# Attention in 16 heads: side work dealt out between the three fills of a head, and the rows of maxima issued on ScalarE's queue

## The chip, the cores and the metric

The kernel runs on one core of a Trainium2 chip. The metric is the device time in microseconds from start to end of one execution; the time before is the median of three runs.

## The reference, cut to what matters

The whole program is two transformer-like layers over x of shape (16, 512, 256). The change touches only the second layer's attention (16 batches, 512 tokens, 16 heads of width 16):

```python
h = _layernorm(x) * (1 + ca) + sa
qkv = (h @ w_qkv).reshape(Bx, Tx, 3, H, HD)
scores = einsum('bhqd,bhkd->bhqk', q, k) * SCALE      # causal mask to -inf
scores = scores + head_scales * (q[..., :8] @ dir) * (k[..., :8] @ dir)
attn = softmax(scores); out = attn @ v
x = x + ga * (out @ w_out)
```

## The kernel before, in words

`attention_stage` writes one program for each engine by hand; the engines meet only at semaphores, and each executes its own list in order. `Signal` objects count events: `pe.wait_ge(*ex(b, k))` waits for the k-th exponential of batch b. The batch loop (`pe_batch`, `dve_batch`, `act_batch`, `sp_batch`) is unrolled for batch 0, looped over batches 1 to 13 and unrolled for 14 and 15. In batch i the 16 heads h run one after the other, and each head has three **fills** f = 0, 1, 2 (512, 512 and 256 columns of scores).

For each fill TensorE (PE) does `pe_scores` (L1275 and the mask L1277) of head h, with key tokens on the partitions, and then `pe_max` (L1257 and the mask L1259) of head h + 7 (`AHEAD`), with query tokens on the partitions. VectorE (DVE) reduces the latter to row maxima (`dve_max`, L1483, four reductions per head); ScalarE (ACT) exponentiates the former (`act_exp`, L1610, three per head). The max banks are two, so `pe_max` of a fill waits for the reduction of the fill two before it; the score banks are three, so `pe_scores(h, f)` waits for the exponential of fill f of head h - 1.

Heads go in **groups** of four. When the maxima of a group are there, PE turns them (`pe_turn_max`, L1323), DVE writes their negative in two bf16 parts (`dve_neg_max`, L1499 and L1501, tile `neg_top`), and two DMAs of 4 KB each, the **row** DMAs (`sp_row`, L1765), put them into two partitions of `q_stack`, from where the next group's `pe_scores` adds them. In the third fill of heads 0, 4, 8, 12 PE also multiplies the last group's probabilities by the values (`pe_pv`, L1293).

Between heads stands the **side work** of the neighbouring batches: for batch i + 1 the q and k products (`pe_qk`, after heads 0 and 1), which ACT and DVE split into three bf16 parts with POOL (`act_qk` L1645, `dve_qk_rest` L1522, `act_qk2` L1649, `pool_qk3` L1710); the values (after head 3); for batch i - 1 the normalising of the outputs (`dve_normal`), the splitting of the turned outputs (`dve_o_lo`), the output product (`pe_out`, after heads 8 and 9), `act_delta` and the addition to x (`dve_add`, L1534); for batch i + 2 the layer norm (`dve_stats`, `dve_norm`, `act_hT`, `dve_hT_lo`).

SyncE (SP) moves the parts: `sp_store` (L1747) writes them to DRAM in twelve DMAs, and `sp_load(i + 1, g)` (L1759) brings group g of q and k into `q_stack` and `k_stack` in six. A load waits until the group's heads of batch i have been scored, and load 0 also until all twelve stores have landed. `pe_max` of head 0 of batch i + 1, which stands in head 9 of batch i, waits for load 0.

Of the kernel before, what the change touches and what calls it, by code (L numbers as in the profile page):

```python
# [27 lines left out]
P = 128  # L28
NB = 16
# [1137 lines left out]
def attention_stage(nc, t, ps, mem):  # L1167
# [7 lines left out]
    with ExitStack() as ctx:  # L1175
# [179 lines left out]
        def pe_batch(pe, i, first, last, turn):  # L1355
            for h in range(HEADS):
# [9 lines left out]
                if h % GROUP == 1 and not (last and h + GROUP > HEADS):  # L1366

                    g = h // GROUP
                    if g:
                        pe.wait_ge(*oe(i, g))  # L1370
                    else:
                        pe.wait_ge(*(neg(i, N_SHIFT) if first else oe(i - 1, NG)))
                    pe_turn_max(pe, *((i, g + 1) if g + 1 < NG else (i + 1, 0)))
# [83 lines left out]
        def dve_stats(dve, b):  # L1457
            for n in range(TT):
                tile = x[:, bass.ds(b * TT + n, 1), :].rearrange("p a d -> p (a d)")
                dve.bn_stats(stats[:, n, :], tile).then_inc(s_stat.sem, 1)  # L1460
            for n in range(TT):
# [6 lines left out]
        def dve_norm(dve, b, first=False):  # L1468
            if not first:
                dve.wait_ge(*lnt(b - 1, DK))  # L1470
            dve.wait_ge(*s_pow(b, 1))
            for n in range(TT):
# [13 lines left out]
        def dve_hT_lo(dve, b):  # L1486
            for k, f in enumerate((1, 0)):
# [37 lines left out]
        def dve_o_lo(dve, b):  # L1525
            for f in range(DK):
# [9 lines left out]
        def dve_batch(dve, i, first, last, norm):  # L1536
            for h in range(HEADS):
                if h == 15 and norm:
                    dve_max(dve, i + 1, h + AHEAD - HEADS, (0, 1))
                    dve_hT_lo(dve, i + 2)  # L1540
                    dve_max(dve, i + 1, h + AHEAD - HEADS, (2,))
                elif h + AHEAD < HEADS:
                    dve_max(dve, i, h + AHEAD)
                elif not last:
                    dve_max(dve, i + 1, h + AHEAD - HEADS)
                if h % GROUP == 1 and not (last and h + GROUP > HEADS):
                    g = h // GROUP
                    dve_neg_max(dve, *((i, g + 1) if g + 1 < NG else (i + 1, 0)))
                if h in (0, 1) and not last:
                    for n in range(2):  # L1550
                        dve_qk_rest(dve, i + 1, 2 * h + n)
                if h == 4 and not first:
                    dve_normal(dve, i - 1, 3, SIDE_B)
                if h == 6 and not first:
                    dve_o_lo(dve, i - 1)
                if h == 7:
                    dve_normal(dve, i, 0, SIDE_B)
                if h == 10:
                    dve_normal(dve, i, 1, SIDE_A)
                    if not first:  # L1560
                        dve_add(dve, i - 1, 0)
                if h == 11 and not first:
                    dve_add(dve, i - 1, 1)
                if h == 8 and norm:
                    dve_stats(dve, i + 2)
                if h == 12 and norm:
                    dve_norm(dve, i + 2)
                if h == 13:
                    dve_normal(dve, i, 2, SIDE_A)

        @block.vector
        def _(dve):
            dve_stats(dve, 0)
            dve_norm(dve, 0, True)
            dve_hT_lo(dve, 0)
            dve_stats(dve, 1)
            dve_norm(dve, 1)
# [22 lines left out]
        def act_exp(act, b, h, first):  # L1600


            g = h // GROUP - (1 if h % GROUP == 0 else 0)
            if g > 0:
                act.wait_ge(*pv(b, g))
            elif not first:
                act.wait_ge(*pv(b - 1, NG + g))
            for f, w in enumerate((512, 512, 256)):
                act.wait_ge(*stp(b, 3 * h + f + 1))
                act.activation(probs[:, slot(h), 512 * f:512 * f + w], bank(f)[:, 0:w], ACT.Exp).then_inc(ex.sem, 1)  # L1610
# [7 lines left out]
        def act_values(act, b):  # L1618
            for n in range(2):
# [6 lines left out]
        def act_hT(act, b):  # L1626
            for k, f in enumerate((1, 0)):
                act.wait_ge(*lnt(b, k + 1))
                if k == 0 and not (isinstance(b, int) and b == 0):
                    act.wait_ge(*q3(b - 1, 4))  # L1630
                act.nop(nofuse=True)
                act.activation(hT[:, f, :], bank((SIDE_A, SIDE_B)[f]), ACT.Identity,
                               bias=mod[:, SHIFT_A + f, bass.ds(b, 1)],
                               scale=mod[:, SCALE_A + f, bass.ds(b, 1)]).then_inc(hTf.sem, 1)
            for k, f in enumerate((1, 0)):
                act.wait_ge(*hTf(b, k + 1))
                if k == 0 and not (isinstance(b, int) and b == 0):
                    act.wait_ge(*vp(b - 1, 2))
# [987 lines left out]
```

## Time and profile before

| | before |
|---|---|
| median of 3 runs | 2698.3 us (2697.41 to 2700.79) |
| profiled execution: its own time | 2689.7 us |
| span of that execution | 2687.9 us |
| PE busy over the span | 2297.5 us (85%) |
| DVE, ACT, POOL busy | 1619.2, 1319.7, 483.9 us (60%, 49%, 18%) |
| mean granted TensorE clock | 0.927 |
| attention's batch loop | about 1163 to 2160 us of the span |

Busy shares are means over stages with different limits; only the attention stage is touched. A matmul's row in a timeline can overlap its neighbour's, as matmuls are pipelined, so the distance between starts tells more than durations.

### The profile page before, as it was taken

To read this page: it belongs to the slowest core of one execution; us is meant where nothing else is said; L and a number is where in the kernel's file an instruction comes from. 1 tells how busy PE (TensorE), PEld (TensorE's weight loads), DVE (VectorE), ACT (ScalarE), POOL (GpSimd) and SP (SyncE) were. 2 spreads that over 40 slices of the span, in tenths; PEclk is the share of its full clock that TensorE was granted. 3 is DMA by queue.
4 is the path that set the end of the run, shared out by engine and by line. 5 is a ranking of instruction groups with operands and counts; after the bars stand their busy time and mean duration, and the time that the engine had idled before them with its cause. 6 is when DMAs were issued, how large, how long until landed. Compare 5 with 4: busy or idle time off the path is not lost. (4 is left out here: it accounts for less than half of the span.)

```text
span 2687.9 us, 45298 instructions
## 1 busy us (share of the span) xinstructions
PE 2297.5 (85%) x15010; PEld 1685.1 (63%) x15010; DVE 1619.2 (60%) x3537; ACT 1319.7 (49%) x2260; POOL 483.9 (18%) x397
## 2 busy tenths in 40 slices
PE   7999999999699997378888888888888875169997
PEld 6666666666588886245555555555555565158996
DVE  4667766765454443456666666666666655766664
ACT  3555565555455556235555555555555543034442
POOL 0011011100011116100000011111000022036664
PEclk8999999999799997679999999999999987579998
DMA  4200000000100000222322232233322228245542
GB/s 112 87 0 0 0 0 0 0 0 0 32 0 0 0 0 24 67 70 74 78 73 72 71 80 72 72 75 78 81 73 71 49 87 279 52 127 124 127 93 32
DMA packets 122975, 156.64 MB, mean 58 GB/s; under 512 B 26896, under 2 KB 104096, under 8 KB 122784
## 3 DMA queue, kind: packets, MB, share of 16 engines
q1 hardware_dynamic: 108576, 130.38, 17.7%
q0 software_dynamic: 14336, 25.44, 4.8%
q8 instruction: 38, 0.62, 0.1%
q14 instruction: 25, 0.20, 0.0%
HBM read 96.26 MB, written 58.98 MB: 58 GB/s over the span
## 5 line engine op out<-in xcount | busy, mean ns | idle before, releaser
L1483 DVE TENSOR_REDUCE at_top<-psum 128x1 f32<-128x512 f32 (+3 forms) x1024 | 446.7, 483 | 302.4 <-PE psum L1259 301.8
L1610 ACT ACTIVATE at_probs<-psum 128x512 f32<-128x512 f32 (+1 forms) x768 | 365.8, 530 | 347.8 <-PE psum L1277 345.5
L1257 PE MATMUL psum<-at_k_stack,at_q_stack 96*128 96x512 bf16 (+3 forms) x1024 | 296.1, 316 | 127.4 <-DMA at_k_stack<-qk_parts 71.9
L1275 PE MATMUL psum<-at_q_stack,at_k_stack 98*128 98x512 bf16 (+3 forms) x1024 | 289.9, 310 | 23.5 <-ACT at_probs L1610 16.8
L1257 PEld LDWEIGHTS psum<-at_k_stack,at_q_stack 96*128 96x128 bf16 x1024 | 103.3, 101 | 228.4 <-DVE at_top L1483 101.7
L1259 PE MATMUL psum<-at_mask_q,at_ident_b 128*128 128x128 bf16 x1024 | 206.9, 228 | 0.0
L1277 PE MATMUL psum<-at_mask_k,at_ident_b 128*128 128x128 bf16 x1024 | 202.9, 224 | 0.0
L1275 PEld LDWEIGHTS psum<-at_q_stack,at_k_stack 98*128 98x128 bf16 x1024 | 102.8, 100 | 116.3 <-issue 44.7
L1293 PE MATMUL psum<-at_probs,at_values 128*32 128x512 f32 (+3 forms) x2048 | 151.1, 436 | 0.9 <-ACT at_probs L1610 0.9
L2334 POOL DMA_INDIRECT out<-ex_result,slot_tokens x64 | 119.6, 1869 | 103.8 <-DVE ex_result L2466 89.2
L2512 ACT ACTIVATE ex_mid<-psum,ex_b_up 128x512 f32<-128x512 f32 x96 | 66.2, 690 | 106.2 <-PE psum L61 104.1
L334 PE MATMUL psum<-h_taps,w_conv 128*64 128x512 f32 x512 | 113.5, 595 | 0.0
L1293 PEld LDWEIGHTS psum<-at_probs,at_values 128*32 128x32 f32 x2048 | 60.0, 109 | 81.7 <-issue 62.9
L59 PE MATMUL psum<-ex_w_down_hi,ex_mid_hi 128*128 128x256 f32 x384 | 108.9, 284 | 0.3 <-DVE ex_mid_lo L2445 0.3
L61 PE MATMUL psum<-ex_w_down_hi,ex_mid_lo 128*128 128x256 f32 x384 | 107.5, 280 | 0.0
L60 PE MATMUL psum<-ex_w_down_lo,ex_mid_hi 128*128 128x256 f32 x384 | 107.5, 280 | 0.0
L59 PE MATMUL psum<-hT_hi,w_in_hi 128*128 128x512 f32 x256 | 102.0, 398 | 3.5 <-DVE hT_lo L444 3.5
L1277 PEld LDWEIGHTS psum<-at_mask_k,at_ident_b 128*128 128x128 bf16 x1024 | 103.4, 101 | 1.3
L1259 PEld LDWEIGHTS psum<-at_mask_q,at_ident_b 128*128 128x128 bf16 x1024 | 104.0, 102 | 0.0
L60 PE MATMUL psum<-hT_lo,w_in_hi 128*128 128x512 f32 x256 | 101.8, 398 | 0.0
L61 PE MATMUL psum<-hT_hi,w_in_lo 128*128 128x512 f32 x256 | 101.6, 397 | 0.0
L537 DVE RECIPROCAL std<-std 128x512 f32<-128x512 f32 x16 | 53.7, 3353 | 77.9 <-ACT std L654 77.9
(401 smaller groups left out, 5896.5 us busy)
## 6 DMA issues: line engine op xcount, KB each, us to landing
qk_parts<-at_q_parts SPq DMA_DIRECT2D x96, 128.0 KB
qk_parts<-at_k_parts SPq DMA_DIRECT2D x96, 128.0 KB
at_q_stack<-qk_parts SPq DMA_DIRECT2D x64, 192.0 KB
at_k_stack<-qk_parts SPq DMA_DIRECT2D x64, 192.0 KB
x_residual<-in_x SPq DMA_DIRECT2D x16, 512.0 KB, 3.8
at_q_stack<-qk_parts SPq DMA_DIRECT2D x64, 128.0 KB
at_k_stack<-qk_parts SPq DMA_DIRECT2D x64, 128.0 KB
token_rows<-ro_h_tok SPq DMA_DIRECT2D x16, 512.0 KB, 3.0
```

What stands on the lines that cost most here:

```text
L59: pe.matmul(out, w[0], x[0], start=start, stop=False)
L60: pe.matmul(out, w[0], x[1], start=False, stop=False)
L61: return pe.matmul(out, w[1], x[0], start=False, stop=stop)
L334: last = pe.matmul(bank(CONV + m)[side, :], w_conv[:, 2 * IK * g + 2 * m + k, :], h_st[:, m, g, 1 + 2 * k:1 + 2 * k + T], start=(k == 0), ...
L1257: pe.matmul(out, q_stack[0:STACK, h, qt * P:(qt + 1) * P], k_stack[0:STACK, h, 0:w], start=True, stop=True)
L1259: last = pe.matmul(bank(MAX0 + n % 2)[:, col + w - P:col + w], ident_b[:, :], mask_q[:, :], start=False, stop=True, skip_group_check=True)
L1275: pe.matmul(bank(bk)[:, col:col + w], k_stack[0:STACK + N_SHIFT, h, kt * P:(kt + 1) * P], q_stack[0:STACK + N_SHIFT, h, kt * P:T], start=T ...
L1277: last = pe.matmul(bank(bk)[:, col:col + P], ident_b[:, :], mask_k[:, :], start=False, stop=True, skip_group_check=True)
L1293: last = pe.matmul(bank(PV_BANK)[32 * hh:32 * hh + 32, kt * P:T], values[:, kt, GROUP * g + hh, :], probs[:, slot(GROUP * g + hh), P_COL[k ...
L1483: dve.tensor_reduce(top[:, h, qt:qt + 1], bank(MAX0 + n % 2)[:, col:col + w], AX.X, ALU.max).then_inc(mxr.sem, 1)
L1610: act.activation(probs[:, slot(h), 512 * f:512 * f + w], bank(f)[:, 0:w], ACT.Exp).then_inc(ex.sem, 1)
L2334: pool.indirect_dma_start(out=rows_out, out_offset=bass.IndirectOffsetOnAxis(ap=index[:, e, c * TT + a:c * TT + a + 1], axis=0), in_=resul ...
```

## The change

Three things change. First, `act_batch` and `dve_batch` loop over the fills inside a head, and side operations that stood together between two heads are dealt out one per fill, some a head later than before. Second, the row DMAs are issued by ACT (`act_row`) in the first fill of heads 2, 6, 10 and 14 (for batch 0's first group before the loop), and SP's list holds stores and loads alone; `sp_load(·, 1)` gets a wait for row DMA 2 of the batch before. Third, on PE `pe_turn_max` moves ahead of the third fill of heads 1, 5, 9, 13, and the second `pe_turn_delta` from after head 11 to after head 12. No operation is added or removed.

```diff
@@ PE
-                if h % GROUP == 1 and not (last and h + GROUP > HEADS):
+                    if f == 1 and h % GROUP == 1 and not (last and h + GROUP > HEADS):
...
-                if h == 11 and not first:
+                if h == 12 and not first:
                     pe.wait_ge(*xs(i - 1, 1))
                     pe_turn_delta(pe, i - 1, 1)
@@ DVE
+                for f in range(3):
+                    if h + AHEAD < HEADS:
+                        dve_max(dve, i, h + AHEAD, (f,))
...
+                    if h == 1 and f < 2 and not last:
+                        dve_qk_rest(dve, i + 1, f)
+                    if h == 2 and f > 0 and not last:
+                        dve_qk_rest(dve, i + 1, 1 + f)
...
+                    if h == 6 and f > 0 and not first:
+                        dve_o_lo(dve, i - 1, (f - 1,))
...
+                    if (h, f) == (11, 0):
+                        dve_normal(dve, i, 1, SIDE_A)
+                    if (h, f) == (11, 1) and not first:
                         dve_add(dve, i - 1, 0)
...
+                    if (h, f) == (13, 0) and not first:
+                        dve_add(dve, i - 1, 1)
+                    if h == 12 and f > 0 and norm:
+                        dve_norm(dve, i + 2, False, (2 * f - 2, 2 * f - 1))
...
+                    if h == 15 and f in (0, 2) and norm:
+                        dve_hT_lo(dve, i + 2, (f // 2,))
@@ ACT
+        def act_row(act, b, g):
+            act.wait_ge(*neg(b, N_SHIFT * (g + 1)))
+            for j in range(N_SHIFT):
+                act.dma_start(q_stack[STACK + j:STACK + j + 1, GROUP * g:GROUP * (g + 1), :].rearrange(
+                    "a h (q p) -> a (h q) p", p=P), neg_top[:, j, :]).then_inc(row[g].sem, 16)
...
+                for f in range(3):
+                    act_exp(act, i, h, f, first)
...
+                    if h == 1 and not last:
+                        if f < 2:
+                            act_qk(act, i + 1, f)
+                        else:
+                            act_qk2(act, i + 1, 0)
+                    if f == 0 and h % GROUP == 2 and not (last and h + GROUP > HEADS):
+                        g = h // GROUP
+                        act_row(act, *((i, g + 1) if g + 1 < NG else (i + 1, 0)))
+                    if h == 2 and f < 2 and not last:
+                        if f == 0:
+                            act_qk2(act, i + 1, 1)
+                        act_qk(act, i + 1, 2 + f)
+                    if h == 3 and f < 2 and not last:
+                        act_qk2(act, i + 1, 2 + f)
...
+                        if (h, f) == (14, 1):
+                            act_hT(act, i + 2, 0)
+                        if (h, f) == (14, 2):
+                            act_hT_hi(act, i + 2, 0)
+                        if (h, f) == (15, 0):
+                            act_hT(act, i + 2, 1)
+                        if (h, f) == (15, 1):
+                            act_hT_hi(act, i + 2, 1)
@@ SP
             if g == 0:
                 sp.wait_ge(*stored(b, stored.per))
+            elif g == 1 and not (isinstance(b, int) and b == 0):
+                sp.wait_ge(*row[2](b - 1, row[2].per))
...
-        def sp_batch(sp, i, last):
-            sp_row(sp, i, 1)
-            if not last:
-                sp_store(sp, i + 1, 0)
-                sp_store(sp, i + 1, 1)
-            sp_row(sp, i, 2)
-            if not last:
-                sp_load(sp, i + 1, 0)
-                sp_load(sp, i + 1, 1)
-            sp_row(sp, i, 3)
...
+        def sp_batch(sp, i):
+            for side in range(2):
+                sp_store(sp, i + 1, side)
+            for g in range(NG):
+                sp_load(sp, i + 1, g)
```

On ACT, heads 0 to 2 of batch 0 (the loop has the same order). Before, `at_q_parts<-psum` and `at_k_parts<-psum` are `act_qk`, the rows that read `at_hT` are `act_qk2`, and `at_probs` are the exponentials, 512, 512 and 256 wide:

```order
L1645 ACTIVATE at_q_parts<-psum 128x512 x2
L1649 ACTIVATE at_q_parts<-at_hT 128x512 x2
L1610 ACTIVATE at_probs<-psum 128x512 x2
L1610 ACTIVATE at_probs<-psum 128x256
L1645 ACTIVATE at_k_parts<-psum 128x512 x2
L1649 ACTIVATE at_k_parts<-at_hT 128x512 x2
```

The changed kernel at the same place, from head 1's first exponential to head 2's second:

```order
L1618 ACTIVATE at_probs<-psum 128x512
L1661 ACTIVATE at_q_parts<-psum 128x512
L1618 ACTIVATE at_probs<-psum 128x512
L1661 ACTIVATE at_q_parts<-psum 128x512
L1618 ACTIVATE at_probs<-psum 128x256
L1665 ACTIVATE at_q_parts<-at_hT 128x512
L1618 ACTIVATE at_probs<-psum 128x512
L1623 DMA at_q_stack<-at_neg_top 1x16x128 x2
L1665 ACTIVATE at_q_parts<-at_hT 128x512
L1661 ACTIVATE at_k_parts<-psum 128x512
L1618 ACTIVATE at_probs<-psum 128x512
L1661 ACTIVATE at_k_parts<-psum 128x512
```

The q operations moved from ahead of head 1's exponentials to among and behind them, the k operations from ahead of head 2's to among head 2's and 3's, and the two row DMAs now stand on ACT.

On SP, the start of the loop body: stores (`qk_parts<-`), row DMAs (`at_q_stack<-at_neg_top`), and the first DMA of load 0 (`at_q_stack<-qk_parts`). Before:

```order
L1765 DMA at_q_stack<-at_neg_top 1x16x128 x2
L1743 ISA
L1744 ISA
L1747 DMA qk_parts<-at_q_parts 8x16x512 x6
L1744 REGISTER_ALU
L1747 DMA qk_parts<-at_k_parts 8x16x512 x6
L1763 REGISTER_ALU
L1765 DMA at_q_stack<-at_neg_top 1x16x128 x2
L1752 ISA
L1754 ISA
L1759 DMA at_q_stack<-qk_parts 48x1x2048
```

After:

```order
L1784 ISA
L1787 DMA qk_parts<-at_q_parts 8x16x512 x6
L1784 REGISTER_ALU
L1787 DMA qk_parts<-at_k_parts 8x16x512 x6
L1792 ISA
L1794 ISA
L1801 DMA at_q_stack<-qk_parts 48x1x2048
```

Load 0 now follows the stores directly; the row DMA pair of group 2, issued after head 5's maxima, no longer stands ahead of it.

On DVE, heads 11 to 13 of the loop in the changed kernel (RECIPROCAL and `at_o_tok` are `dve_normal`, `x_residual` is `dve_add`, the reductions are the maxima):

```order
L1485 TENSOR_REDUCE at_top<-psum 128x1
L1513 RECIPROCAL at_recip<-psum 128x16
L1516 TENSOR_TENSOR at_o_tok<-psum,at_recip 128x4x64
L1482 REGISTER_ALU
L1485 TENSOR_REDUCE at_top<-psum 128x1 x2
L1537 ISA
L1537 TENSOR_TENSOR x_residual<-x_residual,psum 128x512
```

Before, these three side operations stood together between the maxima of heads 10 and 11; now the normalising stands behind the first fill of head 11 and the addition behind its second.

## Rows read from the trace of the kernel before

**Rows 1.** Busy time in 13 periods of the batch loop (span, then each engine)

```profile
1236.10:2067.40 831.30, 726.41 (x6351) 480.59 (x6350) 533.61 (x1340) 450.74 (x911) 85.79 (x78) 0.96 0.30 74
```

**Rows 2.** Waits of PE, 1220 to 2130 us: total, times, longest

```profile
PE psum L1257 <- DMA at_k_stack<-qk_parts: 46.4, 14, 3.8
PE psum L1257 <- DVE at_top L1483: 46.3, 70, 1.0
PE psum L1275 <- ACT at_probs L1610: 16.6, 28, 1.1
```

**Rows 3.** PE's timeline around the wait in head 9 (start, us)

```profile
1772.95 0.39 PE L1275 MATMUL psum<-at_q_stack,at_k_stack 98*128 98x512 bf16 x1
...
1777.19 0.39 PE L1257 MATMUL psum<-at_k_stack,at_q_stack 96*128 96x512 bf16 x1 [3.79 <-DMA at_k_stack<-qk_parts]
```

**Rows 4.** Windows before and behind that wait; the clock is third from the end

```profile
1756.50:1773.10 16.60, 15.48 (x158) 9.63 (x157) 11.94 (x32) 8.46 (x18) 0.00 (x0) 1.00 0.43 83
1777.10:1781.50 4.40, 4.31 (x21) 2.94 (x21) 2.23 (x6) 0.98 (x2) 0.00 (x0) 0.63 0.14 54
```

**Rows 5.** Waits of SP's queue, 1220 to 2130 us

```profile
SPq L1765 <- DVE at_neg_top L1501: 420.3, 58, 9.6
```

**Rows 6.** SP's timeline in the same batch: load 2 of the batch before; stores; rows; loads

```profile
1722.05 1.90 SPq L1759 DMA_DIRECT2D at_q_stack<-qk_parts  x3
...
1747.54 3.78 SPq L1747 DMA_DIRECT2D qk_parts<-at_q_parts  x6
1751.55 3.77 SPq L1747 DMA_DIRECT2D qk_parts<-at_k_parts  x6
1762.71 1.21 SPq L1765 DMA_DIRECT2D at_q_stack<-at_neg_top  x2
1764.12 1.95 SPq L1759 DMA_DIRECT2D at_q_stack<-qk_parts  x3
...
1767.58 1.83 SPq L1759 DMA_DIRECT2D at_q_stack<-qk_parts  x3
```

**Rows 7.** SP's timeline at the start of the stage: store of k, then load 0

```profile
1121.56 3.83 SPq L1747 DMA_DIRECT2D qk_parts<-at_k_parts  x6
1128.84 1.95 SPq L1759 DMA_DIRECT2D at_q_stack<-qk_parts  x3
```

**Rows 8.** Windows at the end of load 2; the last column is GB/s

```profile
1730.00:1732.00 2.00, 2.00 (x22) 1.59 (x20) 1.93 (x7) 0.86 (x2) 0.00 (x0) 1.00 0.11 45
1732.00:1734.00 2.00, 2.00 (x21) 1.46 (x19) 1.64 (x5) 2.00 (x5) 0.00 (x0) 1.00 0.02 4
```

**Rows 9.** ACT's and POOL's timelines, heads 1 to 3 of the same batch

```profile
1749.42 0.63 ACT L1649 ACTIVATE at_k_parts<-at_hT 128x512 bf16<-128x512 f32 x1 [0.24 <-DVE at_hT L1522]
1749.95 2.63 ACT L1610 ACTIVATE at_probs<-psum 128x512 f32<-128x512 f32 x6
...
1749.26 2.27 POOL L1710 TENSOR_TENSOR at_k_parts<-at_hT,at_k_parts 128x512 bf16<-128x512 f32 x2 [3.10 <-ACT at_k_parts L1649]
```

**Rows 10.** PE's timeline: head 2's start, and side waits of heads 2, 7, 13, 15

```profile
1747.87 0.39 PE L1275 MATMUL psum<-at_q_stack,at_k_stack 98*128 98x512 bf16 x1
...
1750.04 0.28 PE L1257 MATMUL psum<-at_k_stack,at_q_stack 96*128 96x256 bf16 x1 [0.59 <-DVE at_top L1483]
...
1766.87 0.28 PE L1257 MATMUL psum<-at_k_stack,at_q_stack 96*128 96x256 bf16 x1 [0.91 <-DVE at_top L1483]
...
1793.13 0.28 PE L1257 MATMUL psum<-at_k_stack,at_q_stack 96*128 96x256 bf16 x1 [1.01 <-DVE at_top L1483]
...
1799.29 0.39 PE L1275 MATMUL psum<-at_q_stack,at_k_stack 98*128 98x512 bf16 x1 [0.97 <-ACT at_probs L1610]
```

**Rows 11.** DVE's timeline: one head's reductions, then an addition to x

```profile
1785.23 1.67 DVE L1483 TENSOR_REDUCE at_top<-psum 128x1 f32<-128x512 f32 x4
1786.91 0.69 DVE L1534 TENSOR_TENSOR x_residual<-x_residual,psum 128x512 f32 x1
```

**Rows 12.** Wait of PE in batch 0's head 9 (1203 to 1213 us)

```profile
PE psum L1257 <- DMA at_k_stack<-qk_parts: 7.2, 1, 7.2
```

More of the change, by code:

```diff
@@ L1466, in dve_stats, with dve_norm @@
             dve.tensor_scalar(var_eps[:, :], moments[:, :, 1], EPS, None, ALU.add).then_inc(s_eps.sem, 1)
-        def dve_norm(dve, b, first=False):
-            if not first:
+        def dve_norm(dve, b, first=False, tiles=range(TT)):
+            if not first and tiles[0] == 0:
                 dve.wait_ge(*lnt(b - 1, DK))
             dve.wait_ge(*s_pow(b, 1))
-            for n in range(TT):
+            for n in tiles:
                 tile = x[:, bass.ds(b * TT + n, 1), :].rearrange("p a d -> p (a d)")
@@ L1484, in dve_max, with dve_hT_lo @@
                                       ALU.max).then_inc(mxr.sem, 1)
-        def dve_hT_lo(dve, b):
-            for k, f in enumerate((1, 0)):
+        def dve_hT_lo(dve, b, steps=range(DK)):
+            for k in steps:
+                f = 1 - k
                 dve.wait_ge(*hTh(b, k + 1))
@@ L1523, in dve_qk_rest, with dve_o_lo @@
                               ALU.subtract).then_inc(qr.sem, 1)
-        def dve_o_lo(dve, b):
-            for f in range(DK):
+        def dve_o_lo(dve, b, fs=range(DK)):
+            for f in fs:
                 dve.wait_ge(*yh(b, f + 1))
@@ L1537, in dve_batch @@
             for h in range(HEADS):
[L1538 to L1560, printed above, removed]
-                        dve_add(dve, i - 1, 0)
@@ L1576, in _ @@
             dve_stats(dve, 1)
+            dve_moments(dve, 1)
             dve_norm(dve, 1)
@@ L1649, in act_qk2, with act_o_hi @@
             act.activation(qk_parts[n // 2][:, 1, n % 2, :], rest[:, n % 2, :], ACT.Copy).then_inc(q2.sem, 1)
-        def act_o_hi(act, b):
-            for f in range(DK):
+        def act_o_hi(act, b, fs=range(DK)):
+            for f in fs:
                 act.wait_ge(*yp(b, f + 1))
@@ L1663, in act_batch @@
             for h in range(HEADS):
-                act_exp(act, i, h, first)
-                if h % GROUP == 0 and not (first and h == 0):
-                    act_keep_oT(act, *((i, h // GROUP - 1) if h else (i - 1, NG - 1)))
-                if h in (0, 1) and not last:
-                    for n in range(2):
-                        act_qk(act, i + 1, 2 * h + n)
-                    for n in range(2):
-                        act_qk2(act, i + 1, 2 * h + n)
-                if h == 3 and not last:
-                    act_values(act, i + 1)
@@ L1681, in _ @@
         @block.scalar
         def _(act):
-            act_hT(act, 0)
+            for k in range(DK):
+                act_hT(act, 0, k)
+            for k in range(DK):
+                act_hT_hi(act, 0, k)
             for m in range(2):
@@ L1689, in _ @@
             act_values(act, 0)
-            act_hT(act, 1)
+            for k in range(DK):
+                act_hT(act, 1, k)
+            for k in range(DK):
+                act_hT_hi(act, 1, k)
+            act_row(act, 0, 0)
             act_batch(act, 0, True, False, True)
```

121 lines of the change are left out of this document (62 added, 59 removed).

## The prediction

> **What bounds the kernel now.** I read the busy times of the batch loop first, then who waits for whom, then the timelines. Over 13 periods PE is busy 726 of 831 us and DVE 534, ACT 451 [rows 1]: a period is 63.9 us, and PE is the engine that sets it. The reader is to see that no other engine comes near, so only PE's idle time can be won: 105 us of 831, 8.1 us a period, and what the clock loses (0.96 on the mean).
>
> PE's waits show where it lies [rows 2]: 46.4 us on DMA in 14 waits (3.3 us each, once a batch), 46.3 us on row maxima in 70 short waits, 16.6 us on exponentials in 28. The DMA wait is one place: head 9 starts at 1772.95, and its first `pe_max` runs at 1777.19, when load 0 of the next batch has landed [rows 3]. Ahead of it the granted clock is 1.00, behind it 0.63 over 4.4 us [rows 4], that is, mostly the 1.2 GHz level: (1 - 0.63) x 4.4 = 1.6 us more.
>
> Why is load 0 late? SP waits 420 us for `neg_top`, 58 times [rows 5]. In the batch shown it issues the k store at 1751.55 and stands from 1755.3 to 1762.7 before the row DMAs of group 2, and only then, at 1764.12, issues load 0 [rows 6]. It lands 13.0 us later. At the start of the stage no row stands between: load 0 is issued 7.3 us after the k store's start [rows 7]. By that the stores had landed at about 1751.55 + 7.3 = 1758.9, so SP's list holds load 0 back by 5.2 us.
>
> **Removed on SP.** With the rows gone, load 0 goes when the stores have landed. But the stores start later, since the k parts are made later. Before, the last `act_qk2` starts at 1749.42, ahead of the exponentials of heads 2 and 3 [rows 9]; now it stands behind head 3's second fill. I step through heads 1 to 3, with 0.5 us for each 512-wide ACT operation back to back (six exponentials, two of them half as wide, in 2.63 [rows 9]), 0.6 for an `act_qk2`, and 1.7 us for a head's matmuls or its four reductions [rows 11]:
> - Head 1: `pe_qk` of k waits for the first `dve_qk_rest`, now behind two more exponentials' turns; about 0.5 us in place of the present wait before it. Head 2 starts at about 1747.7 (1747.87 before [rows 10]).
> - Head 2 on ACT: first exponential to 1748.6, the two row DMAs, `act_qk2`, `act_qk`, second exponential. With 0.6 us for the DMAs (below) it ends near 1750.9, while PE wants it for head 3's second fill at about 1749.9: a wait of 1.0. The third exponential costs 0.35 more, and head 3's last `pe_max` waits 0.6 for DVE, which now has two `dve_qk_rest` in head 2. Gone are the waits of head 2's third fill (0.6 [rows 10]) and about 0.4 behind it. Head 4 starts some 0.8 us later than now.
> - The last `act_qk2` then ends near 1754.1. POOL adds 1.2 (two in 2.27 [rows 9]), so the k store starts near 1755.3, against 1751.55, and load 0 goes at 1755.3 + 7.3 = 1762.6: 1.5 us earlier than 1764.12, not 5.2. Most of what SP's list gives is taken back by ACT's.
>
> Heads 4 to 8: the wait of 0.9 in head 7 behind `dve_o_lo` [rows 10] turns into two, as ACT's row DMAs and `act_o_hi` now delay head 6's exponentials; I count 0.2 lost. So PE comes to head 9's `pe_max` at about 1773.2 + 1.0 = 1774.2.
>
> Landing: 13.0 us when load 1 is issued 3.5 us behind [rows 6]. Load 2, alone, goes at 1722.05 and its traffic ends just after 1732 (45 GB/s up to there, 4 behind it [rows 8]), 10.2 us. Load 1 now waits for head 7's scores, some 5 us behind load 0, so it lies between: 1772.8 to 1775.6. PE goes on at 1774.2 to 1775.6; I take 1774.7, a wait of 0.5, too short to pull down the clock (waits of 1 us in heads 7 and 13 [rows 10] are followed by matmuls of full speed). Before it was 1777.19, with a wait of 3.8; for the mean wait of 3.3 the gain is 2.0, and 1.4 of the clock's 1.6. Sum at head 9: 3.4 us a batch, the 1.0 lost on the way already in it.
>
> **Added on ACT: two DMA issues, four times a batch.** No row shows ACT issuing a DMA. On SP a pair takes 1.21 us [rows 6]. Bounds: 0 (issue overlaps the running exponential) and 1.2 us (ACT stands still). I take 0.6, half of a pair beside the exponential ahead of it; both ends are kept for the range. The exponentials of the same head queue behind the pair, and for them `pe_scores` of the next head.
>
> The Trainium skill (Perfetto Trace Analysis, DMA Instruction — HWDGE) speaks against this: the issuing sequencer is free for its next instruction only when its descriptors are generated, which is what the profiled window shows. By that the queue stands for the whole 1.2 us a pair, and the sum below would be some 2 us a batch smaller, about 2675; no run here shows it yet for ACT.
>
> **Dealt out, heads 10 to 0.** The exponential wait of 0.97 in head 15 and the 1.01 in head 13 [rows 10] are the large ones, with 0.4 in head 12. In head 13 `dve_norm` is halved and its second half lies beside `pe_pv`: 1.0 won. In heads 11 and 12, however, a normalising and an addition (0.65 each [rows 11]) now stand between the maxima on which `pe_max` waits two fills later, with less PE work beside them: about 1.0 lost, 0.4 of it there before. At head 15 `act_hT` and its split are dealt among five exponentials, but the row pair joins them: head 0's `pe_pv` waits about 1.1 for the last exponential, as it does now. Together +0.4 in head 13 to 12's exchange, -0.3 for heads 10 and 14 behind the pair: nothing, with bounds of 1.5 either way.
>
> **`pe_turn_max` earlier, `sp_load`'s new wait:** nothing. The maxima turned are a head old; row DMA 2 is issued in head 6 and load 1 waits for head 7's scores anyway, and if that row came later, load 2 behind it on SP has ten microseconds to spare.
>
> **Sum.** 14 batches x 3.4 = 48 us. Batch 0 waits 7.2 [rows 12], but its chain is moved too: 1 us. The profiled execution took 2689.7, so 2641; the median of the runs lies 8.6 above that execution, so 2698.3 - 49, say 2650.
>
> **The rivals.**
> 1. *The side waits go as well* (chance 0.20). If the pair costs ACT next to nothing, the 1.0 in head 3 goes, the store is 0.6 earlier, head 7's and 15's waits shrink: about 2 us a batch more, 14 x 5.4 = 76 us, 2622. For it: PE's short waits all lie behind side work in a lump. Against: DVE has as much to do in a head as PE (1.7 us), so any side operation there is felt.
> 2. *The load stays late* (0.15). The change does on SP what it says, but the parts are finished 1.5 us later than I step through. Load 0 then goes at 1764.1 and lands at 1777.1 as before; what is lost or won in heads 0 to 8 goes into that wait. Time 2685 to 2702, say 2695.
> 3. *ACT becomes the holder: slower* (0.17). A pair holds ACT for 1.2 us or more. Each exponential behind it is late, and PE waits 0.6 more in heads 11, 15 and 0, 1.1 to 1.5 a batch; the k parts are later by 1 to 2 us more, so load 0 goes after 1764.12 and lands 0.5 to 1 us later than now. 14 x 2 = 28 us: 2725. The point that decides: whether load 0 is issued later than 16.2 us after head 2's start (1764.12 - 1747.87).
>
> The forecast has 0.48.
>
> **How the numbers follow.** The forecast's own range is 2632 to 2678 (the pair at 0 to 1.2 us). The range for 8 in 10 leaves out the lower half of rival 1 and most of rival 3: 2618 to 2704. This measurement tells a change from none at about 0.2%, 5.4 us. Faster: the forecast, rival 1 and a third of rival 2, 0.73. Same: half of rival 2 and a little of 3, 0.10. Slower: 0.17.
>
> **What would show it.** Right: the DMA wait of `pe_max` in head 9 falls from 46 us to under 15 over the loop; load 0 is issued 14 to 15.5 us after head 2's start; PE's clock behind head 9 is 1.00; a new wait on ACT's exponentials of about 1 us stands in head 3; the period is near 60.5 us. Wrong on the size: a pair on ACT's queue of 0.1 or of more than 1.2 us, or exponentials that start while the pair is being issued. Wrong on the mechanism: the DMA wait keeps its 3 us, or moves to another load.

## The result, and the profile after

| | before, same comparison | after |
|---|---|---|
| median | 2697.41 us (2691.75 to 2700.79, 5 runs) | 2717.1 us (2714.58 to 2724.2, 5 runs) |
| ratio, 95% interval | | 1.008 [1.0063, 1.0097] |
| profiled execution: own time, span | 2689.7, 2687.9 us | 2721.45, 2719.7 us |
| mean granted clock | 0.927 | 0.920 |

The change makes the kernel 0.8% slower, 20 us by the medians and 32 by the two profiled executions. The prediction was 2650 us, with 2618 to 2704 as its range.

Busy time over 13 periods of the changed kernel, the answer to [rows 1]:

```profile
1239.93:2096.73 856.80, 752.63 (x6347) 478.75 (x6346) 534.41 (x1340) 444.76 (x911) 86.58 (x78) 0.94 0.30 72
```

A period is 65.9 us against 63.95. PE is busy 26 us longer with the same matmuls (6347 records against 6351), at a mean clock of 0.94 against 0.96, while its idle time is the same: 104 us against 105. So the loss shows as slow matmuls, not as waiting. Where PE waits, 1220 to 2150 us (total, times, longest), against [rows 2]:

```profile
PE psum L1275 <- DMA at_q_stack<-at_neg_top: 34.5, 15, 3.4
PE psum L1257 <- DVE at_top L1485: 32.1, 58, 0.7
PE psum L1275 <- ACT at_probs L1618: 18.3, 40, 0.8
PE psum L59 <- DVE at_hT L1525: 8.3, 14, 0.6
```

The wait of `pe_max` for load 0, 46.4 us before, is gone from the list. The waits on maxima fell from 46.3 to 32.1 us. In their place stands a DMA wait that was 1.2 us in 2 waits before: `pe_scores` (L1275) waits for the row DMAs (`at_q_stack<-at_neg_top`), 34.5 us in 15 waits, once a batch. SP's timeline in one batch, against [rows 6]: both stores, then load 0, with no row between; load 1 follows once row pair 2 has landed.

```profile
1765.56 3.73 SPq L1787 DMA_DIRECT2D qk_parts<-at_q_parts  x6
1769.44 4.08 SPq L1787 DMA_DIRECT2D qk_parts<-at_k_parts  x6
1777.62 1.91 SPq L1801 DMA_DIRECT2D at_q_stack<-qk_parts  x3
1779.58 1.53 SPq L1801 DMA_DIRECT2D at_k_stack<-qk_parts  x3
1786.46 1.83 SPq L1801 DMA_DIRECT2D at_q_stack<-qk_parts  x3
```

PE's timeline of the same batch, from the start of head 2 to the start of head 9:

```profile
1761.89 0.39 PE L1275 MATMUL psum<-at_q_stack,at_k_stack 98*128 98x512 bf16 x1
...
1786.57 0.60 PE L1275 MATMUL psum<-at_q_stack,at_k_stack 98*128 98x512 bf16 x1 [3.28 <-DMA at_q_stack<-at_neg_top]
...
1789.02 4.26 PE L1293 MATMUL psum<-at_probs,at_values 128*32 128x512 f32 x32
...
1795.01 0.39 PE L1275 MATMUL psum<-at_q_stack,at_k_stack 98*128 98x512 bf16 x1
```

Load 0 goes 15.7 us after head 2's start (16.25 before). At 1783.3 PE stops before the first scores of head 8, for 3.28 us. Behind that stop the same 32 products of probabilities and values that take 2.36 us elsewhere take 4.26. The row pair that is waited for is the one that ACT issues in head 6; ACT's timeline there:

```profile
1778.15 0.60 ACT L1618 ACTIVATE at_probs<-psum 128x512 f32<-128x512 f32 x1 [1.42 <-PE psum L1277]
1778.23 1.16 ACTq L1623 DMA_DIRECT2D at_q_stack<-at_neg_top  x2
1779.51 0.60 ACT L1670 ACTIVATE at_o_hi<-psum 128x512 fp32r<-128x512 f32 x1 [0.76 <-issue]
```

It is issued 0.6 us behind load 0, while SP is still issuing the rest of it. The time from issue to landing of this pair (two DMAs, so the smallest and largest value are the two), as the tile's view gives it, and behind it that of the pair issued in head 2 of the same batch, when no load is in flight:

```profile
DMA to landing us min/median/max: 2.3/5.0/7.7
```

```profile
DMA to landing us min/median/max: 1.7/1.7/1.8
```

4 KB that land in 1.8 us by themselves take 7.7 us here: from the second DMA's issue, about 1778.8, that is 1786.5, just where PE's stop ends. The windows ahead of the stop, across it, and behind it (the clock is third from the end, the last column GB/s):

```profile
1780.00:1784.00 4.00, 2.39 (x18) 1.22 (x18) 3.26 (x7) 2.61 (x7) 0.00 (x0) 1.00 0.71 140
1781.00:1786.00 5.00, 1.67 (x15) 0.92 (x12) 2.39 (x6) 1.61 (x5) 0.00 (x0) 1.00 0.59 118
1786.50:1793.20 6.70, 6.63 (x44) 2.71 (x44) 2.66 (x7) 1.19 (x2) 0.00 (x0) 0.52 0.49 100
```

The pair is in flight together with load 0, while the DMA engines move 118 to 140 GB/s; behind the stop the clock is at its 1.2 GHz level (0.52) for 6.7 us. Before, [rows 4] showed 0.63 over 4.4 us.

### The profile page after: what moved, and what is told of

Its sections match the earlier page's. It is cut to its first block and busy times, and to the rows that moved or that the text cites. A ratio compares the mean times of both kernels' runs of the same rounds, so it can differ in the third digit from the quotient of the medians.

```text
span 2719.7 us, 45305 instructions
## 1 busy us (share of the span) xinstructions
PE 2327.7 (86%) x15010; PEld 1681.6 (62%) x15010; DVE 1620.2 (60%) x3537; ACT 1311.9 (48%) x2260; POOL 485.0 (18%) x397
## 5 line engine op out<-in xcount | busy, mean ns | idle before, releaser
L1485 DVE TENSOR_REDUCE at_top<-psum 128x1 f32<-128x512 f32 (+3 forms) x1024 | 457.1, 484 | 370.0 <-PE psum L1259 369.6
L1618 ACT ACTIVATE at_probs<-psum 128x512 f32<-128x512 f32 (+1 forms) x768 | 385.7, 536 | 455.4 <-PE psum L1277 453.9
L1275 PE MATMUL psum<-at_q_stack,at_k_stack 98*128 98x512 bf16 (+3 forms) x1024 | 289.4, 309 | 65.6 <-DMA at_q_stack<-at_neg_top 44.7
L1275 PEld LDWEIGHTS psum<-at_q_stack,at_k_stack 98*128 98x128 bf16 x1024 | 101.6, 99 | 164.2 <-issue 78.0
L1293 PE MATMUL psum<-at_probs,at_values 128*32 128x512 f32 (+3 forms) x2048 | 165.6, 467 | 0.9 <-ACT at_probs L1618 0.9
```

Of the source, the lines that this page charges most:

```text
L1275: pe.matmul(bank(bk)[:, col:col + w], k_stack[0:STACK + N_SHIFT, h, kt * P:(kt + 1) * P], q_stack[0:STACK + N_SHIFT, h, kt * P:T], start=T ...
L1293: last = pe.matmul(bank(PV_BANK)[32 * hh:32 * hh + 32, kt * P:T], values[:, kt, GROUP * g + hh, :], probs[:, slot(GROUP * g + hh), P_COL[k ...
L1485: dve.tensor_reduce(top[:, h, qt:qt + 1], bank(MAX0 + n % 2)[:, col:col + w], AX.X, ALU.max).then_inc(mxr.sem, 1)
```

## The experiments

To see where a batch gains and loses, I took the distances between the first scores matmuls of successive heads from PE's timelines, as means over 12 batches, and added them up in four stretches (us; they sum to the period; a distance counts for the head at whose start it begins, so the stop ahead of head 8 is in head 7). The last column is the ratio of times to the kernel before in the same comparison. "Row 2" stands for the pair of row DMAs of group 2.

```
                                     heads 1-3  4-6   7-9   10-0  period  ratio [95%]
before                                 12.68    8.94  17.36 24.94  63.9
after                                  14.14    9.15  17.19 25.35  65.8   1.008  [1.0063, 1.0097]
e1 row 2 ahead of load 0               14.69    9.15  18.77 25.41  68.0   1.0193 [1.0171, 1.0216]
e2 dealt out, rows on SP as before     12.85    9.16  18.17 24.60  64.8   1.0037 [1.0026, 1.0048]
e3 not dealt out, rows on ACT          13.10    8.94  15.05 25.78  62.9   0.9955 [0.9938, 0.9972]
e4 after, q/k work in lumps            14.27    9.15  12.73 25.33  61.5   0.9865 [0.9844, 0.9885]
e5 e4, heads 10 to 12 as before        13.36    9.16  13.17 24.33  60.0   0.9814 [0.9797, 0.983]
e6 before, load 0 ahead of row 2 (SP)  12.69    8.94  18.63 24.64  64.9   1.0064 [1.0047, 1.0081]
e7 e5's dealing, rows on SP as e6      12.50    9.15  18.07 23.92  63.6   1.0003 [0.9991, 1.0015]
e8 e6, row 2 alone on ACT              12.68    8.94  16.33 24.64  62.6   0.9928 [0.9915, 0.9942]
e9 e7, row 2 alone on ACT              12.49    9.15  15.41 23.92  61.0   0.9842 [0.9828, 0.9855]
```

My theory was that row 2, issued into load 0's traffic, lands late and stops PE in head 8, and that this alone eats what the removed wait brought. The rival was that the dealing and the issues on ACT lose the time, wherever PE happens to wait for it. I call them the first and the second theory.

**e1_row_first.** Load 0 also waits until row 2 has landed; everything else as in the changed kernel.

```diff
             if g == 0:
                 sp.wait_ge(*stored(b, stored.per))
-            elif g == 1 and not (isinstance(b, int) and b == 0):
-                sp.wait_ge(*row[2](b - 1, row[2].per))
+                if not (isinstance(b, int) and b == 0):
+                    sp.wait_ge(*row[2](b - 1, row[2].per))
```

> The changed kernel, but load 0 also waits until the row DMAs of group 2 have landed. Theory 1 (collision): the row pair issued in head 6 lands late because load 0's packets fill the DMA engines; then here it lands in about 2 us, PE's wait at the start of head 8 (3.3 us) goes with the slow clock behind it, but load 0 is issued some 3 us later and the old wait in head 9 returns with 3 to 5 us: 2680 to 2700 us. Theory 2 (ACT): what costs is the issuing and the dealing on ScalarE, and the row pair is slow because ACT issues it; then it lands late here too and the time is 2717 or more.

Measured: 2749.17 us, ratio 1.0193. The pair goes ahead of load 0 and lands in 1.8 us; the wait of head 8 is gone, and the one of head 9 is back. Timelines of ACT's and SP's queues, PE's waits of 1240 to 2100 us, and head 8's products with the values, at full speed again:

```profile
1730.88 1.15 ACTq L1623 DMA_DIRECT2D at_q_stack<-at_neg_top  x2
...
1733.21 1.91 SPq L1801 DMA_DIRECT2D at_q_stack<-qk_parts  x3
```

```profile
PE psum L1257 <- DMA at_k_stack<-qk_parts: 58.3, 13, 5.0
```

```profile
1737.09 2.36 PE L1293 MATMUL psum<-at_probs,at_values 128*32 128x512 f32 x32
```

This shows what makes the pair late: the load in front of it. The time I had expected (2680 to 2700) was too good: the load wait is now 4.5 us a batch, longer than before's 3.3. Load 0 is issued when the pair has landed, 2.3 us behind the pair's own issue, and that is 18.7 to 20.2 us after head 2's start, where it was 16.25 before. It is the pair that sets this and not the stores, which in the changed kernel, where they start at the same place, have landed by 15.7 us. The pair is issued when DVE has written `neg_top`, and ahead of that heads 2 and 3 take 9.3 us together, 7.3 before. Head 3 also ran at the low clock in 8 of the 12 batches, 1.5 us longer each time.

**e2_dealt_sp_rows.** The dealing alone, with the changed kernel's order on PE: rows on SP, in the old order.

```diff
-                    if f == 0 and h % GROUP == 2 and not (last and h + GROUP > HEADS):
-                        g = h // GROUP
-                        act_row(act, *((i, g + 1) if g + 1 < NG else (i + 1, 0)))
...
+            sp_row(sp, i, 2)
+            if not last:
+                sp_load(sp, i + 1, 0)
+                sp_load(sp, i + 1, 1)
+            sp_row(sp, i, 3)
```

> Side work dealt out as in the changed kernel, the rows issued by SP in the old order. Theory 1: row pair of group 2 ahead of load 0, so no wait in head 8 and the load wait in head 9 is back with about 3 us; dealing by itself costs 1 to 2 us a batch against before (head 3's wait): 2700 to 2720 us. Theory 2: dealing and issuing both cost ACT; without the pairs on ACT the waits on exponentials in heads 3 and 7 shrink by 0.5 us each: 2690 or less.

Measured: 2704.08 us, ratio 1.0037, as the first theory had it. Dealing costs 0.85 us a batch: heads 10 to 0 gain 0.34, heads 7 to 9 lose 0.81, since load 0 is later. PE's load wait over 1240 to 2100 us is 3.8 us a time:

```profile
PE psum L1257 <- DMA at_k_stack<-qk_parts: 49.0, 13, 4.2
```

**e3_lumps_act_rows.** The rows on ACT alone: side work as before, each pair issued behind the first exponential of heads 2, 6, 10, 14.

```diff
+                if f == 0 and h % GROUP == 2 and not (last and h + GROUP > HEADS):
+                    r = h // GROUP
+                    act_row(act, *((b, r + 1) if r + 1 < NG else (b + 1, 0)))
...
+            elif g == 1 and not (isinstance(b, int) and b == 0):
+                sp.wait_ge(*row[2](b - 1, row[2].per))
...
+        def sp_batch(sp, i):
+            for side in range(2):
+                sp_store(sp, i + 1, side)
+            for g in range(NG):
+                sp_load(sp, i + 1, g)
```

> The kernel before, with only the row DMAs moved to ScalarE (between the first and second exponential of heads 2, 6, 10, 14) and SP's list of stores and loads alone. The q and k parts are made early, so load 0 can go about 5 us earlier than before. Theory 1: load 0 has passed its densest phase when the row pair is issued, head 8 waits 0 to 1.5 us, head 9 not at all: 2640 to 2660 us. Theory 2: four pairs on ACT's queue at 1.2 us each delay exponentials on PE's path: 2700 us or more, with waits on exponentials in heads 3, 7, 11.

Measured: 2680.45 us, ratio 0.9955: faster than before, by less than the first theory wanted. Since the stores are early, the pair (1757.21) comes 5.0 us behind load 0 (1752.25), and lands in 5.0 us:

```profile
1757.21 1.18 ACTq L1603 DMA_DIRECT2D at_q_stack<-at_neg_top  x2
```

```profile
PE psum L1275 <- ACT at_probs L1616: 29.3, 41, 1.7
PE psum L1275 <- DMA at_q_stack<-at_neg_top: 5.9, 11, 1.4
```

The row wait is 0.5 us a time, but the wait for head 15's last exponential at the start of head 0, 0.97 us in [rows 10], is now 1.65, and heads 10 to 0 are 0.84 us longer. So the second theory has a part in it: the issues on ACT have a price. Head 8 takes 6.84 us on the mean against 5.42 before, with the same matmuls, so low clock takes another part.

**e4_qk_lumps.** The changed kernel with the q/k operations of ACT and DVE in lumps behind heads 0 and 1, so that only the stores and load 0 come earlier.

```diff
-                    if h == 1 and f < 2 and not last:
-                        dve_qk_rest(dve, i + 1, f)
-                    if h == 2 and f > 0 and not last:
-                        dve_qk_rest(dve, i + 1, 1 + f)
+                    if h in (0, 1) and f == 2 and not last:
+                        for n in range(2):
+                            dve_qk_rest(dve, i + 1, 2 * h + n)
...
+                    if h in (0, 1) and f == 2 and not last:
+                        for n in range(2):
+                            act_qk(act, i + 1, 2 * h + n)
+                        for n in range(2):
+                            act_qk2(act, i + 1, 2 * h + n)
```

> The changed kernel, with the q and k operations of ACT and VectorE back behind heads 0 and 1 in lumps, all else dealt out and the rows on ScalarE. Theory 1: load 0 goes some 5 us earlier against the row pair than in the changed kernel, the waits in heads 8 and 9 go, and the rest of the dealing costs 0 to 1 us a batch: 2650 to 2670 us. Theory 2: about as the changed kernel, 2710 us.

Measured: 2658.62 us, ratio 0.9865, as the first theory had it. ACT still issues every pair, DVE still has the dealt work of heads 5 to 15, and 58 us are back: heads 7 to 9 take 12.73 us against 17.19. Load 0 goes at 1737.42, row 2 6.8 us later:

```profile
1744.25 1.15 ACTq L1622 DMA_DIRECT2D at_q_stack<-at_neg_top  x2
```

```profile
PE psum L1275 <- DMA at_q_stack<-at_neg_top: 5.0, 5, 1.5
```

**e5_heads10_12.** e4, and the normalising, both additions and the second `pe_turn_delta` where they stood before.

```diff
-                    if (h, f) == (11, 0):
+                    if (h, f) == (10, 2):
                         dve_normal(dve, i, 1, SIDE_A)
-                    if (h, f) == (11, 1) and not first:
+                    if (h, f) == (10, 2) and not first:
                         dve_add(dve, i - 1, 0)
-                    if (h, f) == (13, 0) and not first:
+                    if (h, f) == (11, 2) and not first:
                         dve_add(dve, i - 1, 1)
```

> The kernel of e4 with heads 10 to 12 as before: VectorE's normalising and the two additions behind heads 10 and 11, and TensorE's second turning of delta after head 11; the layer norm stays dealt out in head 12. Both theories on the collision leave this open. If the short waits of heads 11 and 12 come from the place of these operations, head 12 falls from 5.55 to about 4.0 us, head 11 rises from 1.68 to 2.4, and the period falls by 0.5 to 0.8 us: 2645 to 2652 us. If they come from ScalarE, nothing changes: 2658.

Measured: 2639.39 us (2638.01 to 2643.42), ratio 0.9814: the fastest version, faster than both kernels, and faster than expected (2645 to 2652). Head 12 fell from 5.55 to 3.97 us and head 11 rose from 1.68 to 2.28. With smaller changes in heads 13, 15 and 0, heads 10 to 0 are 1.0 us shorter. Head 3 fell too (6.35 to 5.44), with no edit near it: at the low clock it takes 6.7 us and at full clock 5.2, and it ran low in 2 of 12 batches where it had in 9. That part of the gain, 0.9 us a batch, is not explained by the edit. Its periods:

```profile
1240.00:2080.00 840.00, 769.62 (x6852) 500.44 (x6851) 571.07 (x1428) 476.85 (x973) 86.66 (x79) 0.99 0.33 78
```

The clock is 0.99, and PE idles 5.0 us a period (70.4 over 14).

**e6_load_ahead.** Does the early load need ACT's queue? The kernel before, with two calls exchanged on SP.

```diff
                 sp_store(sp, i + 1, 1)
+                sp_load(sp, i + 1, 0)
             sp_row(sp, i, 2)
             if not last:
-                sp_load(sp, i + 1, 0)
                 sp_load(sp, i + 1, 1)
```

> The kernel before with one call of SyncE moved: load 0 is issued ahead of the row DMAs of group 2 instead of behind them; nothing on ScalarE, VectorE or TensorE changes. Theory 1 (what counts is where load 0 stands against this row pair): load 0 goes about 4 us earlier, the wait in head 9 goes, the row pair is issued 3 to 4 us behind load 0 and lands in 4 to 6 us, so head 8 waits 0 to 2 us: 2645 to 2675 us, better than e3 by what ScalarE's issuing costs there. Theory 2 (the gain of e3 and e4 needs the rows off SyncE's queue): the pair behind the load on the same queue waits for all of its traffic, head 8 waits 5 us or more: 2700 us or more.

Measured: 2707.56 us, ratio 1.0064. The first theory's time did not come, though the pair stands 3.8 us behind load 0 and not 0.6. It is behind it on the same queue, and it lands 7.0 to 9.1 us after its issue in twelve batches, where the changed kernel has 6.5 to 7.8. A second thing differs: this kernel lacks the changed one's wait of load 1 for row pair 2, and load 1 goes 3.3 us behind the pair, before it has landed.

```profile
1768.19 1.93 SPq L1759 DMA_DIRECT2D at_q_stack<-qk_parts  x3
...
1771.98 1.21 SPq L1765 DMA_DIRECT2D at_q_stack<-at_neg_top  x2
1775.27 1.89 SPq L1759 DMA_DIRECT2D at_q_stack<-qk_parts  x3
```

```profile
PE psum L1275 <- DMA at_q_stack<-at_neg_top: 53.2, 13, 5.1
```

```profile
DMA to landing us min/median/max: 3.7/5.3/7.0
```

**e7_mix.** e5's dealing with e6's order on SP, to have no issue on ACT at all. Against e5:

```diff
-                    if f == 0 and h % GROUP == 2 and not (last and h + GROUP > HEADS):
-                        g = h // GROUP
-                        act_row(act, *((i, g + 1) if g + 1 < NG else (i + 1, 0)))
...
+                sp_store(sp, i + 1, 1)
+                sp_load(sp, i + 1, 0)
+            sp_row(sp, i, 2)
+            if not last:
+                sp_load(sp, i + 1, 1)
```

> The kernel of e5 with the rows issued by SyncE in the order of e6 (load 0 ahead of row pair 2). Against e5 it shows what the four pairs cost on ScalarE: with 0.8 us a pair, of which heads 3, 7, 10 and 0 pass some 0.4 on each, the period is 1.5 us shorter than in e5, unless the row pair lands later on SyncE's queue: 2625 to 2640 us. If issuing on ScalarE costs nothing on TensorE's path: the same as e5.

Measured: 2691.64 us, ratio 1.0003, far from the expected 2625 to 2640. The same wait stands in head 8 (52.4 us in 14), and here too load 1 follows 3.4 us behind the pair. But outside heads 7 to 9 a batch takes 45.57 us against e5's 46.85: 1.28 us is what four pairs on ACT's queue cost PE in e5, 0.86 of it in head 3 (about 0.6 in the batches at full clock, the rest low clock in two of twelve).

**e8_one_pair.** e6, with row 2 alone on ACT. It was meant to change the pair's queue only, but it changes two things: with the pair off SP's list, load 1 also gets the changed kernel's wait until the pair has landed.

```diff
+                if (h, f) == (6, 0):
+                    act_row(act, b, 2)
...
+            elif g == 1 and not (isinstance(b, int) and b == 0):
+                sp.wait_ge(*row[2](b - 1, row[2].per))
...
                 sp_load(sp, i + 1, 0)
-            sp_row(sp, i, 2)
```

> The kernel of e6 (the kernel before, load 0 ahead of row pair 2), with one thing changed: row pair 2 is issued by ScalarE in head 6, the other three stay on SyncE. If the queue is what makes the pair wait for all of load 0, it lands some 9 to 10 us behind load 0's issue in place of 13, head 8 waits 1.5 us or less in place of 4, and heads 1 to 3 and 10 to 0 stay as in the kernel before: period 61.5 us, 2650 to 2665 us. If only the distance between load and pair counts, it lands as in e6 and the time is 2700.

Measured: 2674.16 us, ratio 0.9928. Load 0 and pair have e6's distance (3.9 us), on two queues, and load 1 goes 6.4 us behind the pair, when it has landed:

```profile
1749.95 1.91 SPq L1769 DMA_DIRECT2D at_q_stack<-qk_parts  x3
...
1760.20 1.83 SPq L1769 DMA_DIRECT2D at_q_stack<-qk_parts  x3
```

```profile
1753.84 1.17 ACTq L1603 DMA_DIRECT2D at_q_stack<-at_neg_top  x2
```

```profile
PE psum L1275 <- DMA at_q_stack<-at_neg_top: 15.7, 15, 1.5
```

```profile
DMA to landing us min/median/max: 3.8/4.8/5.8
```

The wait falls from 4.1 us to 1.0 a time, and the kernel by 33 us. How much of this is the queue and how much the held load 1 no run shows. It is slower than I expected because head 8 keeps its low clock (7.37 us, as in e6) behind a wait of only 1 us.

**e9_mix_one_pair.** e7, with row 2 alone on ACT and load 1 held as in e8; it should have joined e5's heads 7 to 9 with e7's rest.

```diff
+                    if (h, f) == (6, 0):
+                        act_row(act, i, 2)
...
                 sp_load(sp, i + 1, 0)
-            sp_row(sp, i, 2)
```

> The dealing of e5 and e7 with row pair 2 on ScalarE and the other three on SyncE. Heads 1 to 3 and 10 to 0 should be those of e7 (45.6 us a batch with heads 4 to 6), heads 7 to 9 those of e5 (13.2 us): period 58.7 us, 2620 to 2630 us. If the clock or the waits move elsewhere, as e5: 2639.

Measured: 2651.06 us, ratio 0.9842, slower than either value expected. The rest is e7's, as expected, but heads 7 to 9 take 15.41 us, not 13.17: the 0.9 us won in head 3 brought row 2 nearer to load 0 (1737.29 and 1733.12, 4.2 us against 5.0), so it lands in 5.6 us, PE waits 1.3 instead of 0.67, and head 8 runs slow (6.91 against 5.64).

## Why the prediction was wrong, point by point

**Removed on SP, load 0.** Right in mechanism, off in size. With the rows gone load 0 goes when the stores have landed; the k store starts 7.55 us after head 2's start (forecast 7.6). But the stores landed 8.2 us after that, not 7.3, so load 0 is 0.5 us earlier instead of 1.5. The load wait of head 9 went all the same: even with the 13.0 us of [rows 6] load 0 would have landed at 1790.6, and PE, stopped ahead of head 8, starts head 9 at 1795.0. Without that stop and the slow matmuls behind it PE would be there at about 1790.1, a wait of 0.5 us at most, as forecast.

**The step that failed.** It is the one under "`sp_load`'s new wait: nothing": "row DMA 2 is issued in head 6 and load 1 waits for head 7's scores anyway, and if that row came later, load 2 behind it on SP has ten microseconds to spare". I asked who waits on SP for row 2, and never when row 2 itself would land once load 0 goes ahead of it, nor that head 8's scores need it. It lands 7.7 us after its issue. PE waits 2.3 us a batch (34.5 in 15) and then runs at 1.2 GHz through `pe_pv`. By the distances of single heads, the stop and the slow matmuls in heads 7 and 8 cost 4.9 us a batch against e1, where neither is (6.64 + 7.41 - 3.76 - 5.41). Before, the load wait and what followed in heads 9 and 10 cost 5.1 against after, which has neither (8.51 + 2.91 - 3.14 - 3.15). One stop took the place of the other, at nearly its price: heads 7 to 9 take 17.19 us after 17.36, where I had forecast about 4 less. e1 changes only the order of load 0 and the pair, and the stop and the slow matmuls behind it are gone. e4, which also moves the q and k work of heads 1 to 3, leaves the pair 6.8 us behind, and there PE waits 5.0 us in all over 1240 to 2100 us. So the cause is shown: load 0, issued just ahead of the pair, makes it late.

**Heads 1 to 3.** Forecast +0.8 us, measured +1.46. Dealing alone costs 0.17 there (e2); the rest, 1.29, comes with the row pair on ACT. It has two parts: in the batches at full clock head 3 takes 6.6 us against e2's 5.8, and in four of twelve it takes 8.0, at a granted clock of 0.79. The pair's net price was mis-sized: it starts 0.08 us into the running exponential and holds ACT's queue 1.16 us, and the next ACT operation starts 1.3 to 1.4 us after that exponential's start where 0.5 was the pace, so 0.8 to 0.9 us net and not 0.6. The Trainium skill (Perfetto Trace Analysis, DMA Instruction — HWDGE) says that the issuing sequencer stands until its descriptors are made; the trace agrees on the 1.16 us, of which the running exponential covers the first part.

**Short waits do not lower the clock.** Wrong too. In head 3 of the changed kernel PE waits 0.74 and then 0.56 us within 2.5 us of time:

```profile
1765.33 0.34 PE L1275 MATMUL psum<-at_q_stack,at_k_stack 98*128 98x384 bf16 x1 [0.74 <-ACT at_probs L1618]
...
1767.14 0.28 PE L1257 MATMUL psum<-at_k_stack,at_q_stack 96*128 96x256 bf16 x1 [0.56 <-DVE at_top L1485]
```

In this batch the matmuls of the values behind it run at full clock. In the next one PE waits the same 0.74 and 0.56 us, and they do not:

```profile
1767.30:1770.20 2.90, 2.90 (x26) 2.86 (x25) 0.78 (x3) 1.02 (x3) 2.12 (x2) 1.00 0.51 167
1834.50:1838.60 4.10, 4.10 (x26) 4.06 (x26) 0.56 (x3) 0.77 (x2) 1.85 (x2) 0.66 0.50 162
```

26 matmuls in 4.10 us instead of 2.90: 1.2 us, in some batches and not in others. Head 8 behind a wait of 1 us (e8) is the same case: it ran slow in 11 batches of 12.

**Heads 10 to 0, "nothing".** Measured +0.41, inside my bounds. Head 12 loses 1.6 and head 13 wins 1.1 by the dealing, as stepped through but larger; e5 shows that the first could be had back without giving up the second (head 12 at 3.97, head 13 at 2.98).

**Sum and rivals.** Over the period: +1.46, +0.21, -0.17, +0.41, that is +1.9 us, and 14 x 1.9 = 27 of the 32 us between the profiled executions. Of the signs that I had listed, the load wait went, the new wait in head 3 was there (0.74 us, listed as about 1), and the clock from head 9 on is 1.00 (1795 to 1805 us), since the slow stretch now lies ahead of it, in head 8. Load 0 was just outside the listed 14 to 15.5 us in the batch shown (15.1 to 15.7 over twelve batches), and the period was not near 60.5. So signs that looked at head 9 alone came true in a slower kernel. The third rival had the right sign and nearly the right time (2725) by another mechanism: its point of decision, load 0 later than 16.2 us after head 2's start, was not reached. It was e5 that came to a period of 60.0 us and to 2639, but by another way than the forecast's: load 0 goes 10.7 us after head 2's start there, not 14 to 15.5, because the q and k work is back in lumps, and row 2 stands some 5 to 7 us behind it.

**What stays open.** Why the low clock comes behind some waits of 0.35 to 1.5 us and not behind others: in e9 head 8 took 5.43 us behind a wait of 1.33 and 7.62 behind one of 0.86. Whether the pair was so late in e6 and e7 because of its queue or because load 1 was issued before it had landed; e6 with load 1 held would tell, and was not run. Whether the rows would do better from a third engine's queue was not tried.

## What to carry to other kernels

When a large transfer is released earlier, list every small DMA that is then issued behind it, and ask for each when it lands and who needs it; being issued early enough is no answer. Put the small urgent one ahead of the load only if the load can still be in time: e1 did it and was the slowest version. Otherwise have the load go as long before the small one as the schedule allows, and hold the next load back until the small one has landed. e8 did that and moved the small one to another queue, and which of the two helped is not shown. After an edit that removes a stop, look at the distance between the two transfers again, since time won ahead of them moves them together.

## What the runs showed of the hardware

A pair of 4 KB DMAs lands in 1.8 us when no load is in flight. With one 768 KB load issued ahead of it, it takes longer. The table has one batch of each run: the distance between the two issues, then from the issue of the pair's second DMA to its landing, then from load 0's issue to that landing (the distance, 0.6 us to the second DMA's issue, and the landing, added), and what this last one is over twelve batches. The last column tells how far behind load 0 the next load is issued; "held" means when the pair has landed.

```
                    pair behind load 0  lands in  after load 0's issue        load 1 behind load 0
on ACT's queue:
  after                    0.6            7.7        8.8  ( 8.0 to  9.7)           held
  e8                       3.9            5.8       10.2  (10.0 to 10.6)           held
  e9                       4.2            5.6       10.3  (10.1 to 10.5)           held
  e3                       5.0            5.0       10.5  (10.4 to 11.0)           held
  e5                       5.0            5.2       10.7  (10.5 to 11.1)           held
  e4                       6.8            4.3       11.7  (10.5 to 11.7)           held
on SP's queue, as load 0:
  e6                       3.8            7.0       11.4  (11.4 to 13.2)            7.1
  e7                       3.8            8.2       12.6  (11.4 to 13.1)            7.2
```

So from ACT's queue a pair that is issued 3.9 us or more behind load 0 lands 10 to 12 us after the load's issue, wherever it stands. That is about when the load's own traffic ends: in e8 (load 0 issued at 1749.95) and in e5 (at 1724.61) the bandwidth in the last column falls away some 10 us after the issue, and the pair lands at 1760.2 and 1735.3. Load 2 alone took 10.2 us before [rows 8]; the 13.0 us of [rows 6] are of a load with a second one 3.5 us behind it.

```profile
1758.00:1760.00 2.00, 0.83 (x6) 0.53 (x6) 1.97 (x6) 0.23 (x1) 0.00 (x0) 0.91 0.13 50
1760.00:1762.00 2.00, 1.70 (x9) 0.99 (x10) 0.46 (x2) 0.60 (x1) 0.00 (x0) 0.50 0.07 8
```

```profile
1733.00:1735.00 2.00, 1.44 (x11) 0.86 (x8) 1.83 (x5) 1.05 (x3) 0.00 (x0) 0.80 0.12 46
1735.00:1737.00 2.00, 1.65 (x8) 0.83 (x8) 0.26 (x1) 0.60 (x1) 0.00 (x0) 0.50 0.08 6
```

A greater distance thus shortens the pair's landing mainly because less of the load is left. In e6 and e7 the pair lands 11 to 13 us after load 0's issue; there it stands on the load's own queue, and load 1 is in flight as well.

The Trainium skill (DMA: Bandwidth & Descriptors, Issuing engines are not separate DMA queues) says that all issuers share the same 16 DMA engines and that issuing from several saves only the sequencer's time. No run here moves the pair to another queue and leaves the rest, so the 33 us between e6 and e8 neither bear this out nor contradict it. The first half of the rule agrees: ACT's queue did not make the pair independent of the load. The same page (Queues, rings and completion order) says that a semaphore's increment lands only after every earlier write of that DMA engine, across its queues; that would explain why a pair on its own queue is late behind a load at all. No run here separates it from plain sharing of the engines.
